# The closing loads of a two-layer mixture-of-experts kernel, issued from two queues instead of one

## The chip, the cores and the metric

The program runs on one core of one Trainium2 chip. The metric is the device time of one execution in microseconds (us), the median of several runs. The engines are TensorE (PE), VectorE (DVE), ScalarE (ACT), GpSimd (POOL) and SyncE (SP). SP computes nothing: it waits on semaphores and issues DMAs. ACT and POOL can issue DMAs too; all of them run on the core's 16 DMA engines.

## The reference

Two layers, each a per-sequence conditioning followed by a mixture of experts, are added to x, which is 4096 tokens of 128 features. The end of the second layer is what matters here. Each token goes to a first and a second choice out of 8 experts, and the two expert rows come back weighted:

```
combine = (g1[:, None] * mask1)[:, :, None] * oh1[:, None, :] + (g2[:, None] * mask2)[:, :, None] * oh2[:, None, :]
expert_out = jnp.einsum('ecf,efh->ech', hmid, w2) + b2[:, None, :]
y = jnp.einsum('nec,ech->nh', combine, expert_out)
shared = jax.nn.silu(x @ sw1 + sb1) @ sw2 + sb2
out = y + SHARED_SCALE * shared
x = x + out
```

## The kernel before

The 4096 tokens lie in SBUF in `acc`, as 32 tiles of 128 tokens. Four tiles make a group, and there are NG = 8 groups. When the expert stage begins, `acc` already holds x and the shared part of the second layer.

The expert stage works on 40 blocks of 256 rows (8 experts, 5 blocks each). PE computes a block, DVE adds the bias into `grp_y` (L1164), and POOL scatters the rows with indirect DMAs (L588) into a DRAM tensor `back1`. It has 4096 rows of first choices and 4096 rows of second choices, in the order of the tokens. The scatters of even blocks count on the semaphore `gy_st[0]`, those of odd blocks on `gy_st[1]`.

The end of the program, which is what is changed, gathers nothing: it reads `back1` in order. It consists of four instruction streams, each in the order in which it is written:

- SP waits until all scatters have landed (L485). Then it issues 16 loads of 256 KB (L488), in the order group 0 first choices, group 0 second choices, group 1 first choices and so on. Both loads of a group g count on one semaphore, `fy_ld[g]`. Behind them SP waits group by group for `f_ac` and issues the 8 stores of `acc` to the output (L491).
- ACT waits for both loads of group g (`fy_ld[g]` at 32) and multiplies the four tiles of second choices by their weights, in place (L764, four ACTIVATEs of 128x128). The last counts on `f_sc`.
- DVE waits for the same semaphore and adds the first choices times their weights to `acc` (L1196, four SCALAR_TENSOR_TENSORs of 128x128). Then it waits for ACT's `f_sc` of this group and adds ACT's four tiles (L1201, one TENSOR_TENSOR of 128x512), which counts on `f_ac`. Only then comes the next group.
- PE and POOL have nothing to do there.

The only other DMA that ACT issues in the whole program is its first, the load of `c0w` (L600). No pool and no scheduler decides anything here: each engine runs its own list.

Of the kernel before, what the change touches and what calls it, by code (L numbers as in the profile page):

```python
# [5 lines left out]
def adaln_moe_two_layers(  # L6
# [44 lines left out]
    S = T // B  # L51
    NSUB = c0_w.shape[0]
    E0, _, F0x2 = f0_gate_up.shape
    F0 = F0x2 // 2
    C0 = F0 // P
    NLANG = c1_b2.shape[0]
    A = c1_w1.shape[1] // NLANG
    E1, _, F1 = f1_w1.shape
    C1 = F1 // P
    TOP_K = 2  # L60
# [8 lines left out]
    NG = NT // G  # L69
# [8 lines left out]
    U = 2  # L78
    UP = U * P
    GPE = CAP // UP  # L80
    NQ = E1 * GPE
# [20 lines left out]
    back1_g = back1.rearrange("(k g i p) h -> k g p i h", p=P, i=G, k=TOP_K)  # L102
# [4 lines left out]
    with ctx:  # L107
        def sb(name, shape, dt=fp32):
            return ctx.enter_context(nc.sbuf_tensor(name, shape, dt))

        def sem(name):
            return ctx.enter_context(nc.semaphore(name))
# [21 lines left out]
        back = [[sb(f"back{k}_{g}", [P, G, H]) for g in range(NG)] for k in range(TOP_K)]  # L134
# [202 lines left out]
        gy_st = [sem(f"gy_st{k}") for k in range(2)]  # L337
# [11 lines left out]
        fy_ld = [sem(f"fy_ld{g}") for g in range(NG)]  # L349
# [25 lines left out]
        def _(sp):  # L375
# [108 lines left out]
            for k in range(2):  # L484
                sp.wait_ge(gy_st[k], 16 * U * (NQ // 2))  # L485
            for g in range(NG):
                for k in range(TOP_K):
                    sp.dma_start(back[k][g][:, :, :], back1_g[k, g]).then_inc(fy_ld[g], 16)  # L488
            for g in range(NG):
                sp.wait_ge(f_ac, g + 1)  # L490
                sp.dma_start(out_g[g], acc[:, g * G:(g + 1) * G, :]).then_inc(o_st, 16)  # L491
# [102 lines left out]
        def _(eng):  # L594
# [104 lines left out]
            for n in range(NG + 2):  # L699
# [9 lines left out]
                if 1 <= n < NG + 1:  # L709
                    k = (n - 1) % 2  # L710
# [47 lines left out]
                q_stage(q, q, last=q == NQ - 1)  # L758


            for g in range(NG):
                eng.wait_ge(fy_ld[g], 16 * TOP_K)
                for i in range(G):
                    ins = sc.activation(back[1][g][:, i, :], back[1][g][:, i, :], ACT.Copy,  # L764
                                        scale=wk[:, 1, g * G + i:g * G + i + 1])
                ins.then_inc(f_sc, 1)
# [438 lines left out]
        def _(pe):  # L1205
# [33 lines left out]
            for n in range(NG + 1):  # L1239
# [11 lines left out]
                if n < NG:  # L1251
                    pe.wait_ge(xT_done, n + 1)
                    if n == 0:
                        pe.wait_ge(ld_c0w, 16)
                        pe.wait_ge(off_ready, 1)
                    _, offs = nc.values_load_multi_w_load_instructions(
                        w0off[0:1, n * GB:(n + 1) * GB], engines=(mybir.EngineType.PE,), min_val=0,
                        max_val=(NSUB - 1) * H, skip_runtime_bounds_check_because="subjects are under NSUB")
                    for b in range(QB):
                        if b == 1 and n >= 3 and n % 2 == 1:  # L1260
                            rank0((n - 3) // 2)
                        for i in range(G):
                            t = i * QB + b
                            last = mm(PS[1 + b][0:S, i * H:(i + 1) * H],  # L1264
                                      xT[n % 2][:, t * S:(t + 1) * S], c0w[:, ds(offs[t], H)],
                                      start=True, stop=True)
                        last.then_inc(pe_c, 1)
# [356 lines left out]
```

## Time and profile before

| | us |
|---|---|
| median of 3 runs | 520.14 |
| lowest and highest run | 518.93 and 521.77 |
| the profiled execution's own time | 520.84 |
| span of the profiled execution, first to last instruction | 518.9 |
| what lies around the span | 1.9 |
| end of the program, from the first closing load (495.54) to the end of the span | 23.3 |

The profile is one execution. Times in its rows are us from the start of the span, and durations marked ns are nanoseconds. A row of the timeline gives the start, the length, the engine, the line, the operation with output and input, the count of instructions merged into the row, and in brackets how long the engine was idle before and what released it. SPq and ACTq are the queues on which SP and ACT issue DMAs: the length of such a row is how long the issue held the issuing engine, not how long the transfer took. PE is busy for 86% of the span as a whole, but that says nothing of the last 25 us, in which it does nothing.

### The profile page before, as it was taken

The numbers are of one execution on the slowest core, as the hardware profiler recorded it, in microseconds if no ns is written. First come the engines' busy times: TensorE is split into PE (matmuls) and PEld (weight loads), VectorE is DVE, ScalarE is ACT, GpSimd is POOL, SyncE is SP. The second block draws the span as 40 slices with busy tenths as digits, with TensorE's granted clock in tenths as the row PEclk, the third lists the DMA queues.
The fourth block names the chain that finished last, engine by engine and source line by source line (L and its number), as shares of the span: only waits on it lengthen the run. The fifth ranks groups of instructions, "written<-read, shape, count | busy, mean of one in ns | idle before, by whom it ended". The sixth has DMA issues, their size and how long they took to land.

```text
span 518.9 us, 10032 instructions
## 1 busy us (share of the span) xinstructions
PE 444.6 (86%) x3126; PEld 383.2 (74%) x3127; DVE 249.5 (48%) x776; ACT 252.7 (49%) x580; POOL 234.3 (45%) x255
## 2 busy tenths in 40 slices
PE   5799788989999989999997899739999999999700
PEld 3688665567777775787876699739999999999700
DVE  1145558856566664255687845303233323332146
ACT  2356662236666653456457334205556555565334
POOL 2006545205555563200646777731565556555600
PEclk8899989999999999999997899959999999999955
DMA  9999981102222214300101111141234333431179
GB/s 235 359 359 342 366 262 41 43 10 78 76 75 73 57 23 142 112 1 1 43 26 42 47 53 46 49 104 42 78 99 143 108 80 110 116 79 31 40 201 287
DMA packets 66129, 58.12 MB, mean 112 GB/s; under 512 B 9484, under 2 KB 53151, under 8 KB 66098
## 3 DMA queue, kind: packets, MB, share of 16 engines
q1 hardware_dynamic: 58402, 44.12, 29.2%
q0 software_dynamic: 7168, 12.56, 7.4%
q10 hardware_dynamic: 528, 1.05, 0.7%
q8 instruction: 17, 0.28, 0.2%
q14 instruction: 14, 0.11, 0.1%
HBM read 30.35 MB, written 29.59 MB: 116 GB/s over the span
## 4 chain that ended last, share of the span: by engine, by line
PE 67%; issue 9%; DVE 8%; POOL 6%; DMA 5%; ACT 3%; SPq 0%; POOLq 0%; DVEq 0%; ACTq 0%
PE PS L1541 14%; PE PS L1207 8%; PE PS L1264 7%; POOL rows L570 5%; PE PS L1465 4%; PE PS L1531 4%; PE PS L1529 4%; PE PS L1530 4%; PE PS L1344 3%; PE PS L1296 3%; PE PS L1305 2%; PE PS L1329 2%; PE PS L1331 2%; PE PS L1330 2%; PE PS L1450 2%
## 5 line engine op out<-in xcount | busy, mean ns | idle before, releaser
L588 POOL DMA_INDIRECT back<-grp_y,grp_i x80 | 79.5, 994 | 72.7 <-DVE grp_y L1164 60.1
L570 POOL DMA_INDIRECT rows<-disp,slot x64 | 63.8, 997 | 65.5 <-DVE slot L1007 46.2
L1541 PE MATMUL PS<-w2r,act 128*128 128x128 f32 x640 | 77.7, 275 | 0.0
L1541 PEld LDWEIGHTS PS<-w2r,act 128*128 128x128 f32 x640 | 74.7, 192 | 0.0
L548 POOL DMA_INDIRECT back<-act,blk_i x48 | 46.9, 976 | 54.2 <-DVE act L960 34.1
L743 ACT ACTIVATE act<-PS,b1r 128x256 f32<-128x256 f32 x160 | 62.8, 475 | 14.6 <-PE PS L1531 14.6
L1164 DVE TENSOR_TENSOR grp_y<-PS,b2r 128x256 f32<-128x256 f32 x40 | 17.0, 425 | 89.7 <-PE PS L1541 84.6
L537 POOL DMA_INDIRECT rows<-disp,slot x32 | 32.0, 1001 | 58.1 <-issue 48.5
L598 ACT ACTIVATE xh<-PS 128x256 fp32r<-128x256 f32 (+1 forms) x48 | 20.1, 419 | 68.5 <-PE PS L1207 68.5
L1529 PE MATMUL PS<-xh,w1h 128*128 128x256 f32 x160 | 48.3, 302 | 0.0
L1531 PE MATMUL PS<-xh,w1l 128*128 128x256 f32 x160 | 45.2, 283 | 0.0
L1530 PE MATMUL PS<-xl,w1h 128*128 128x256 f32 x160 | 44.9, 281 | 0.0
L1264 PE MATMUL PS<-c0w,xT 128*32 x256 | 34.4, 298 | 7.7 <-issue 7.7
L1264 PEld LDWEIGHTS PS<-c0w,xT 128*32 128x32 f32 x256 | 30.0, 121 | 11.1 <-issue 9.3
L695 ACT ACTIVATE act<-PS,sb 128x512 f32<-128x512 f32 x32 | 21.7, 688 | 26.6 <-PE PS L1419 26.2
L1501 PEld LDWEIGHTS PS<-sw,act 128*128 128x128 f32 x256 | 33.7, 214 | 1.2 <-ACT act L695 0.7
L1501 PE MATMUL PS<-sw,act 128*128 128x128 f32 x256 | 34.0, 297 | 0.3 <-DVE acc L1098 0.3
L953 DVE SCALAR_TENSOR_TENSOR act<-PS,blk_x,act 128x256 f32<-128x256 f32 x48 | 23.2, 484 | 20.3 <-ACT act L652 20.3
L1344 PEld LDWEIGHTS PS<-w_dn,act 128*128 128x128 f32 x192 | 26.0, 190 | 9.2 <-issue 8.3
L1344 PE MATMUL PS<-w_dn,act 128*128 x192 | 30.2, 280 | 1.1 <-ACT act L598 1.1
L1530 PEld LDWEIGHTS PS<-xl,w1h 128*128 128x128 f32 x160 | 30.5, 191 | 0.0
L652 ACT ACTIVATE act<-PS,blk_x 128x256 f32<-128x256 f32 x48 | 22.8, 475 | 15.6 <-PE PS L1331 15.6
(237 smaller groups left out, 938.2 us busy)
## 6 DMA issues: line engine op xcount, KB each, us to landing
rows<-zrow SPq DMA_DIRECT2D x32, 260.0 KB, 4.5
grp_x<-rows SPq DMA_DIRECT2D x40, 130.0 KB, 2.4
w_raw<-in_f_gate_up SPq DMA_DIRECT2D x8, 512.0 KB, 9.8
back<-zrow SPq DMA_DIRECT2D x8, 512.0 KB, 7.4
back<-back SPq DMA_DIRECT2D x16, 256.0 KB, 5.1
blk_x<-rows SPq DMA_DIRECT2D x48, 65.0 KB, 1.9
acc<-in_x SPq DMA_DIRECT2D x8, 256.0 KB, 5.6
y0g<-back SPq DMA_DIRECT2D x8, 256.0 KB, 3.1
```

The source lines that it names most:

```text
L548: gp.indirect_dma_start(back0, bass.IndirectOffsetOnAxis(ap=blk_i[c][:, 0:1], axis=0), blk_y[s][:, :], None, bounds_check=last_token, oob_ ...
L570: gp.indirect_dma_start(rows1, bass.IndirectOffsetOnAxis(ap=slot[:, k, t:t + 1], axis=0), disp[:, t, :], None, bounds_check=E1 * CAP - 1, ...
L588: gp.indirect_dma_start(back1, bass.IndirectOffsetOnAxis(ap=grp_i[v % NX][:, u:u + 1], axis=0), grp_y[k][:, u, :], None, bounds_check=last ...
L743: sc.activation(act[k][:, c, 0:UP], PS[1 + k * (C1 // 2) + c // 2][:, (c % 2) * UP:(c % 2 + 1) * UP], ACT.Silu, bias=b1r[e][:, c:c + 1]).t ...
L1207: return nc.tensor.transpose(dst, src, ident[0:k, 0:k])
L1264: last = mm(PS[1 + b][0:S, i * H:(i + 1) * H], xT[n % 2][:, t * S:(t + 1) * S], c0w[:, ds(offs[t], H)], start=True, stop=True)
L1344: last = mm(PS[4 if k == 0 else 7][:, 0:H], blk_aT[k][:, c * P:(c + 1) * P], w_dn[:, ds(off + c * H, H)], start=c == 0, stop=c == C0 - 1)
L1501: last = mm(tile(PS[4], i), tile(act[k][:, c, :], i), sw2[:, c, :], start=c == 0, stop=c == C1 - 1)
L1529: mm(y, high, xh[k][:, 0:UP], start=True, stop=False)
L1530: mm(y, high, xl[k][:, 0:UP], start=False, stop=False)
L1531: last = mm(y, low, xh[k][:, 0:UP], start=False, stop=True)
L1541: last = mm(PS[5 + k][:, u * P:(u + 1) * P], act[k][:, c, u * P:(u + 1) * P], w2r[e][:, c, :], start=c == 0, stop=c == C1 - 1)
```

## The change

SP issues only the eight loads of the first choices. ACT issues the eight loads of the second choices, after it has waited for the same scatters. ACT's eight loads all stand ahead of its first weighting. The semaphores, the sizes, the addresses and the arithmetic are the same.

```diff
             for k in range(2):
                 sp.wait_ge(gy_st[k], 16 * U * (NQ // 2))
             for g in range(NG):
-                for k in range(TOP_K):
-                    sp.dma_start(back[k][g][:, :, :], back1_g[k, g]).then_inc(fy_ld[g], 16)
+                sp.dma_start(back[0][g][:, :, :], back1_g[0, g]).then_inc(fy_ld[g], 16)
             for g in range(NG):
                 sp.wait_ge(f_ac, g + 1)
                 sp.dma_start(out_g[g], acc[:, g * G:(g + 1) * G, :]).then_inc(o_st, 16)
@@ scalar engine, behind the last block of the experts @@
+            for k in range(2):
+                eng.wait_ge(gy_st[k], 16 * U * (NQ // 2))
+            for g in range(NG):
+                eng.dma_start(back[1][g][:, :, :], back1_g[1, g]).then_inc(fy_ld[g], 16)
             for g in range(NG):
                 eng.wait_ge(fy_ld[g], 16 * TOP_K)
```

SP's list at its end before. The rows are the closing loads, two to a group (first and second choices), and the stores.

```order
L488 DMA back_0<-back 128x4x128 x2
L488 DMA back_1<-back 128x4x128 x2
L488 DMA back_2<-back 128x4x128 x2
L488 DMA back_3<-back 128x4x128 x2
L488 DMA back_4<-back 128x4x128 x2
L488 DMA back_5<-back 128x4x128 x2
L488 DMA back_6<-back 128x4x128 x2
L488 DMA back_7<-back 128x4x128 x2
L491 DMA out_x<-acc 128x4x128 x8
```

ACT's list at its end now, from its last work for the experts on. Before, the eight DMA rows were not there, and the ACTIVATE of `back_0` followed the last one of the experts at once.

```order
L742 ACTIVATE act<-PS,b1r 128x256 x8
L763 DMA back_0<-back 128x4x128
L763 DMA back_1<-back 128x4x128
L763 DMA back_2<-back 128x4x128
L763 DMA back_3<-back 128x4x128
L763 DMA back_4<-back 128x4x128
L763 DMA back_5<-back 128x4x128
L763 DMA back_6<-back 128x4x128
L763 DMA back_7<-back 128x4x128
L767 ACTIVATE back_0<-back_0,wk 128x128 x4
L767 ACTIVATE back_1<-back_1,wk 128x128 x4
```

Eight DMAs moved from SP, where each stood in second place of its pair, to ACT, where all of them stand ahead of the weighting of group 0.

## Rows read from the trace of the kernel before

**Rows 1.** Page: span and busy time of the engines.

```profile
span 518.9 us, 10032 instructions
...
PE 444.6 (86%) x3126; PEld 383.2 (74%) x3127; DVE 249.5 (48%) x776; ACT 252.7 (49%) x580; POOL 234.3 (45%) x255
```

**Rows 2.** Chain that ended last, 493 us on: start, length, what.

```profile
493.39 2.09 DMA back<-grp_y,grp_i
...
495.54 0.37 SPq L488
...
495.96 0.50 SPq L488
...
497.05 4.92 DMA back<-back
...
501.99 1.29 ACT back L764 x4
...
503.37 0.69 DVE acc L1201
504.06 1.06 DVE acc L1196 x4
...
514.15 0.69 DVE acc L1201
```

**Rows 3.** Timeline of ACT from 495 us on: groups 0, 1 and 7.

```profile
500.01 1.28 ACT L764 ACTIVATE back<-back,wk 128x128 f32<-128x128 f32 x4 [12.63 <-DMA back<-back]
501.99 1.28 ACT L764 ACTIVATE back<-back,wk 128x128 f32<-128x128 f32 x4 [0.71 <-DMA back<-back]
...
512.56 1.28 ACT L764 ACTIVATE back<-back,wk 128x128 f32<-128x128 f32 x4 [0.28 <-DMA back<-back]
```

**Rows 4.** Views of lines 488, then 491: issue (ns min/median/max), time to landing.

```profile
L488 SPq DMA_DIRECT2D back<-back x16: 366/806/1103, 495.5 to 507.3; - x16
...
DMA to landing us min/median/max: 2.6/5.1/5.5
...
L491 SPq DMA_DIRECT2D out_x<-acc x8: 373/792/922, 508.2 to 514.9; - x8
...
DMA to landing us min/median/max: 3.6/4.4/4.8
```

**Rows 5.** Timeline of SP, single issues: load 5, load 16, store 8.

```profile
497.60 0.86 SPq L488 DMA_DIRECT2D back<-back  x1
...
507.35 0.83 SPq L488 DMA_DIRECT2D back<-back  x1
...
514.87 0.37 SPq L491 DMA_DIRECT2D out_x<-acc  x1
```

**Rows 6.** DMA view: packets started in 495.5:519, 495.5:508.18 and 495.5:504.8, in turn.

```profile
DMA packets 12672, 6.29 MB, mean 268 GB/s; under 512 B 384, under 2 KB 12672, under 8 KB 12672
...
DMA packets 6509, 3.24 MB, mean 255 GB/s; under 512 B 191, under 2 KB 6509, under 8 KB 6509
...
DMA packets 4530, 2.25 MB, mean 242 GB/s; under 512 B 128, under 2 KB 4530, under 8 KB 4530
```

**Rows 7.** Windows of 2 us: the last two columns are DMA share and GB/s.

```profile
495.00:497.00 2.00, 0.00 (x0) 0.00 (x0) 0.00 (x0) 0.00 (x0) 0.00 (x0) 0.50 0.14 37
...
507.00:509.00 2.00, 0.00 (x0) 0.00 (x0) 1.93 (x6) 1.28 (x4) 0.00 (x0) 0.50 1.21 291
...
513.00:515.00 2.00, 0.00 (x0) 0.00 (x0) 1.81 (x6) 0.84 (x3) 0.00 (x0) 0.50 1.15 345
```

**Rows 8.** Timeline of SP, then of ACT, in the first 2 us.

```profile
0.79 0.45 SPq L376 DMA_DIRECT2D acc<-in_x  x1
1.30 0.39 SPq L377 DMA_DIRECT2D w0off<-in_subj  x1
...
0.86 0.86 ACTq L600 DMA_DIRECT2D c0w<-in_c_w  x1
1.76 1.28 ACT L602 ACT_TABLE_LOAD   x1 [0.93 <-issue]
```

## The prediction

> **What bounds the kernel now.** I read the page first: PE is busy 86% of the span [rows 1]. That says nothing of the part that the change touches, so the next view is the chain of waits that ended last, from 493 us on [rows 2]. The reader is to see that PE is gone from it. The last scatter lands, SP issues loads, a group lands at 501.97, ACT weights it, and from 503.37 on the chain runs along DVE without a gap: add ACT's tiles (0.69 us), take the next group's first choices (1.06), and again, up to the add at 514.15. Six periods lie between the adds at 503.37 and 514.15, so one is 10.78 / 6 = 1.80 us. DVE is the bound of that stretch, and ACT is only just ahead of it: ACT waits for a landing before every group [rows 3] and needs 1.28 us of each 1.80.
>
> DMA is nearly a bound too: its engines have a share of 1.15 and more (transfers overlap) at 291 GB/s while loads run and at 345 GB/s once stores do [rows 7]. The last add ends at 514.84, its store is issued at 514.87 [rows 5] and lands 3.6 us later [rows 4], and the span ends at 518.87. The store waits behind two others: a lone transfer of that size takes less (below).
>
> The third view is how long an issue holds the queue. The first issues take 0.37 and 0.50 us [rows 2], but the median of the sixteen is 0.81 [rows 4]: load 5 takes 0.86, and load 16 is held from 507.35 to 508.18 [rows 5]. The packets tell why. All 24 transfers are alike and make 12672 packets, 528 each [rows 6]. When load 16 has been issued (508.18), 16 x 528 - 6509 = 1939 packets are still to be started [rows 6]. I read this as a limit: SP gets rid of a load only when all but some 1930 packets, or 3.7 loads, have been started. That it is the fifth load that first takes longer [rows 5] fits. SP can afford to be held. It computes nothing, and its first store has been ready since 504.06 without setting the end.
>
> **The change part by part.**
>
> *ACT's new wait for the scatters* costs nothing. Behind it stand only the eight loads and the weighting, and ACT is idle for 12.63 us there anyway [rows 3]. SP's same wait ends at 495.5, and ACT's should too.
>
> *SP loses eight issues.* Its first store could go some us earlier than 508.23. It gains nothing at the end: the last store hangs on DVE's last add, and the bytes are the same.
>
> *ACT gains eight issues, ahead of its first weighting.* This is the term that counts. Unlike SP, ACT has work behind its issues, and DVE waits for that work. Before, ACT could start at 500.01. If nothing held it, eight issues of 0.50 + 0.05 us would end at 495.54 + 4.4 = 499.9, just in time. If each queue is held as SP's is now, ACT's eighth load is let go when 8 x 528 - 1930 = 2294 packets of ACT's queue have been started. The two queues share the 16 engines; with equal halves that is 4588 packets in all. In the trace of before 4530 have been started by 504.80 [rows 6], and 58 more take 0.1 us: 504.9. Both queues fill at once now, where SP needed from 495.54 to 495.96 for its second load, so I take off 0.4 for the start: ACT is free at 504.5.
>
> From there by rows: a pause of 0.05, the four ACTIVATEs of group 0 take 1.28 [rows 3], DVE's add starts 0.10 after them (501.99 + 1.28 to 503.37) [rows 2, 3]. That is 505.93, and it ends 0.69 later, at 506.62. DVE has taken group 0's first choices long before. Then seven periods of 1.80 give the end of the last add at 519.22. ACT with 1.28 a group and loads that landed by then stay ahead of DVE, so DVE waits only once, at group 0. Before, this add ended at 514.84: 4.4 us later.
>
> *The last store* wins some back. The stores now come 1.80 us apart with no loads left, and one needs under 0.8 us at 345 GB/s (256 KB), so none queues. The nearest row is the least time to landing of a load, 2.6 us, for the one that met an empty queue [rows 4], against 3.6 of the last store now. I take 2.6, so 1.0 less; the other end is no gain at all, if a write to DRAM takes longer than a read from it. Store issued at 519.25, landed at 521.85, and 0.4 to the end of the span as now (518.87 - 514.87 - 3.6): 522.25, that is 3.4 us more.
>
> *The loads' own rate* is the open price. No row has these loads on two queues. Its bounds are 291 GB/s, as now, and 345, the rate of the stores [rows 7]. By 497 only 0.07 MB have moved (2 us at 37 GB/s) [rows 7]; the other 2.2 MB of the 4588 packets take 6.4 us at 345, which ends at 503.4 instead of 504.9: 1.5 us less. I take the lower rate, since it is measured on the same transfers. A loss is as possible where two queues share unevenly: with 60% for SP's queue ACT would need 2294 / 0.4 = 5735 packets, 2 us later. If ACT's queue is preferred, ACT is free early but the first choices land late. At worst all of ACT's 4224 packets go first, until a little before 504.8; pair 0 then lands near 505.5, DVE needs 1.8 for it, and the first add ends near 507.3, 0.7 later than above.
>
> A rule stands against reading the issues as independent: whether the two issuers hamper each other at the issue itself. In the first 2 us SP issued a small load from 1.30 to 1.69 while ACT's issue ran from 0.86 to 1.72, and neither waited for the other to end [rows 8]. The Trainium skill (Perfetto Trace Analysis, section on the DMA instruction, HWDGE) says that the descriptor generator is locked for exclusive use and that an issue can wait for that lock. By that rule 16 issues of 0.50 us would take turns and end after about 8.5 us, at 504.0; by rows 8 they would not. Either is earlier than the 504.5 of the full queues, so the sum stays.
>
> *Sum.* Span 518.9 + 3.4 = 522.3; with 1.9 around it the profiled execution would go from 520.84 to 524.2. Its own time lies 0.7 above the median of the runs, 520.14, so the forecast for the median is 520.14 + 3.4 = 523.5.
>
> **The rivals.**
>
> 1. *ACT isn't held* (not slower). The eight issues end by 500, before or with the first landing. Against it: SP is held from its fifth load on [rows 5], and nothing in a transfer of the same size on ACT's queue would be different. For it: ACT's one DMA, 1 MB, let it go after 0.86 us and its table load followed at once [rows 8], though that is only one instruction into an empty queue. Then the first pair lands up to 0.4 earlier, DVE's chain moves with it at most, and the DMA engines, busy to the end, give little back: 519.7 to 520.1. The Trainium skill (DMA: Bandwidth & Descriptors, "Issuing engines are not separate DMA queues") says that all issuers share the same 16 engines and that issuing from several saves only the issuer's time. Its result is this rival's, no measurable change, and it says nothing of what the issuer has to do next.
>
> 2. *ACT isn't held and the loads also run at 345 GB/s* (faster). DVE is then the only bound: first landing 499.6, the first add ends about 1.7 later at 501.3 or a little after, seven periods to 513.9, plus 3.0 for the store: 516.9 to 517.3 of span, so 518.1 to 518.6 at the median.
>
> 3. *The limit of 1930 packets is for both queues together*, or SP's queue is preferred (slower still). Then ACT's last load is let go where load 15 or 16 is now, at about 507.3 or at 508.18 [rows 5], 2.8 to 3.7 later than 504.5: 526.3 to 527.2. The rows can't exclude it, as only one queue is ever full in them.
>
> **How the numbers follow.** Main case 0.66, from 522.0 (loads at 345) to 525.5 (60% for SP's queue); rival 3 0.15; rival 1 0.15; rival 2 0.04. The range takes in the main case and rival 3 and leaves rivals 1 and 2 out, 0.19: 521.4 to 527.0. About 0.5%, 2.6 us, is what a measurement of this kernel can tell from no change. Slower by more, above 522.7: rival 3 and four fifths of the main case, 0.68. Within it: the rest of the main case, rival 1 and half of rival 2, 0.30. Faster: 0.02.
>
> **What the profile of the changed kernel would show.** ACT: eight issues from 495.5 on, the first four near 0.5 us, the later ones 1 to 1.8 each, the last ending near 504.5; its first ACTIVATE there and not at 500. It then runs with no wait for a DMA. DVE: first choices of group 0 near 500, then one idle stretch of some 4.5 us before the first add, released by ACT; after it a period of 1.80 and a last add ending near 519.2. Stores land 2.6 to 3 us after issue. The forecast is wrong if ACT's first ACTIVATE comes by 500.5 (rival 1), or after 507 (rival 3), or if the last add doesn't follow ACT's first by 14.7 us.

## The result, and the profile after

The median of 22 runs is 521.53 us against 519.75 us for 22 runs of the kernel before, a difference of 1.8 us. The ratio is 1.004, 95% interval 1.0022 to 1.0058, which is about 2.1 us slower. One run of the changed kernel (528.61) was in a slower state and is left out of the ratio; the median of its other 21 runs is 521.15. The three runs of the kernel before that are shown ahead of the prediction are among its 22 and had a median of 520.14. Timed once more beside the experiments (e9 below), the changed kernel came out at 1.0052 (1.0021 to 1.0084). So the sign was right and the size was a little over half of the 3.4 us forecast.

The length that shows this best is the **closing stretch**: from the issue of the first closing load to the end of the span. It was 518.87 - 495.54 = 23.3 us before. In the profiled execution of the changed kernel (own time 523.92, span 522.0) it is 522.0 - 496.63 = 25.4 us, 2.0 more. That its loads begin 1.1 us later is no part of the change: ahead of them the two programs are the same, and e9 begins them at 493.31.

The timeline from 496 us on, SP and ACT, then DVE's first two and last pieces. It answers to [rows 3] and [rows 2].

```profile
496.63 7.92 SPq L487 DMA_DIRECT2D back<-back  x8
496.64 8.05 ACTq L763 DMA_DIRECT2D back<-back  x8
500.97 1.14 DVE L1199 SCALAR_TENSOR_TENSOR acc<-back,wk,acc 128x128 f32<-128x128 f32 x4 [9.37 <-DMA back<-back]
504.74 7.12 ACT L767 ACTIVATE back<-back,wk 128x128 f32<-128x128 f32 x24 [16.29 <-issue]
506.12 0.69 DVE L1204 TENSOR_TENSOR acc<-acc,back 128x512 f32<-128x512 f32 x1 [4.01 <-ACT back L767]
...
513.64 1.28 ACT L767 ACTIVATE back<-back,wk 128x128 f32<-128x128 f32 x4 [0.29 <-DMA back<-back]
...
518.55 0.69 DVE L1204 TENSOR_TENSOR acc<-acc,back 128x512 f32<-128x512 f32 x1
```

Both loads of group 0 have landed at 500.97, since DVE starts on it there. ACT waits for the same semaphore and doesn't start before 504.74: it is still issuing. DVE then stands idle for 4.01 us before its first add, released by ACT. After that ACT runs 24 ACTIVATEs, six groups, without one wait. The last pair of loads lands at 513.64, 17.0 us after the first issue; in the kernel before it was 512.56 - 495.54 = 17.0 us too [rows 3].

The chain of waits that ended last, in the same stretch. Columns are start, length, what; the group of before is [rows 2].

```profile
498.24 0.53 ACTq L763
...
498.79 1.12 ACTq L763
...
499.94 1.72 ACTq L763
...
501.69 1.56 ACTq L763
...
503.28 1.42 ACTq L763
...
504.74 1.28 ACT back L767 x4
...
506.12 0.69 DVE acc L1204
```

ACT's queue, which wasn't in the chain before, is now the way to the first ACTIVATE. Four issues are free (about 0.5 us each), and the fifth to eighth are held for 1.12, 1.72, 1.56 and 1.42 us.

For comparison, groups 3 and 4 of the kernel before, ACT's weighting and DVE's add:

```profile
505.57 1.28 ACT L764 ACTIVATE back<-back,wk 128x128 f32<-128x128 f32 x4 [0.53 <-DMA back<-back]
506.95 0.69 DVE L1201 TENSOR_TENSOR acc<-acc,back 128x512 f32<-128x512 f32 x1
507.38 1.28 ACT L764 ACTIVATE back<-back,wk 128x128 f32<-128x128 f32 x4 [0.53 <-DMA back<-back]
508.76 0.69 DVE L1201 TENSOR_TENSOR acc<-acc,back 128x512 f32<-128x512 f32 x1
```

There the landings come 1.81 us apart and each add begins 1.38 us after its landing. In the changed kernel DVE has the loads lying ready, and its adds come (518.55 - 506.12) / 7 = 1.78 us apart. So in the kernel before it was the landings that set the pace here, with DVE almost as slow, and a late DVE can make up a little: counted from the first load, its first add is 9.49 - 5.84 = 3.65 us later than before, and its last one ends 3.3 us later.

Packets started in 496:504.7 by queue (q1 is SP's, q10 ACT's), in the form of [rows 6], and two windows, which answer to [rows 7]:

```profile
q1 hardware_dynamic: 2040, 1.02, 44.4%
q10 hardware_dynamic: 1839, 0.92, 41.0%
```

```profile
501.00:503.00 2.00, 0.00 (x0) 0.00 (x0) 1.11 (x4) 0.00 (x0) 0.00 (x0) 0.50 1.21 290
...
513.00:515.00 2.00, 0.00 (x0) 0.00 (x0) 1.93 (x7) 1.62 (x6) 0.00 (x0) 0.50 1.15 345
```

From 501 on, loads on two queues run at 290 GB/s, as on one. When ACT's last issue ended, 4224 - 1839 = 2385 of its packets were still to be started.

The stores' own view, as in [rows 4]:

```profile
L490 SPq DMA_DIRECT2D out_x<-acc x8: 372/373/378, 506.8 to 519.3; - x8
...
DMA to landing us min/median/max: 2.3/3.6/7.2
```

No store is held now, against a median of 0.79 us of issue before. From the end of the last add (519.24) to the end of the span it is 2.8 us, where it was 4.0.

### The profile page after: what moved, and what is told of

Same layout as the page of the kernel before. It is cut to its first block, busy times and chain, and to the rows that moved or that the text cites. A ratio compares the mean times of both kernels' runs of the same rounds, so it can differ in the third digit from the quotient of the medians.

```text
span 522.0 us, 10033 instructions
## 1 busy us (share of the span) xinstructions
PE 445.2 (85%) x3126; PEld 383.5 (73%) x3127; DVE 249.2 (48%) x776; ACT 251.9 (48%) x580; POOL 234.7 (45%) x255
## 4 chain that ended last, share of the span: by engine, by line
PE 68%; issue 9%; DVE 8%; POOL 5%; DMA 4%; ACT 3%; ACTq 2%; POOLq 0%; SPq 0%; DVEq 0%
PE PS L1544 14%; PE PS L1210 8%; PE PS L1267 7%; POOL rows L569 5%; PE PS L1468 4%; PE PS L1534 4%; PE PS L1532 4%; PE PS L1533 4%; PE PS L1347 4%; PE PS L1299 3%; PE PS L1332 2%; PE PS L1308 2%; PE PS L1334 2%; PE PS L1333 2%; PE PS L1453 2%
## 5 line engine op out<-in xcount | busy, mean ns | idle before, releaser
L1267 PEld LDWEIGHTS PS<-c0w,xT 128*32 128x32 f32 x256 | 30.0, 121 | 12.2 <-issue 10.3
L956 DVE SCALAR_TENSOR_TENSOR act<-PS,blk_x,act 128x256 f32<-128x256 f32 x48 | 23.2, 484 | 20.5 <-ACT act L651 20.4
L1532 PEld LDWEIGHTS PS<-xh,w1h 128*128 128x128 f32 x160 | 30.4, 190 | 0.0
```

Of the source, the lines that this page charges most:

```text
L1267: last = mm(PS[1 + b][0:S, i * H:(i + 1) * H], xT[n % 2][:, t * S:(t + 1) * S], c0w[:, ds(offs[t], H)], start=True, stop=True)
L1532: mm(y, high, xh[k][:, 0:UP], start=True, stop=False)
```

## The experiments

Two theories were tested. **Theory 1**: the loss is that ACT comes late to group 0, because its queue holds it while it issues, and DVE waits for it. **Theory 2**: two queues slow the loads themselves. Closing stretch, first weighting and last add are read from each profile, counted in us from the issue of the first closing load.

| kernel | first weighting | last add ends | closing stretch | ratio to before (95%) |
|---|---|---|---|---|
| before | 4.5 | 19.3 | 23.3 | |
| changed | 8.1 | 22.6 | 25.4 | 1.004 (1.0022 to 1.0058) |
| changed again (e9) | 7.9 | 22.4 | 25.1 | 1.0052 (1.0021 to 1.0084) |
| one queue, ACT busy 4.9 us (e1) | 4.8 | 19.3 | 23.0 | 0.9989 (0.9957 to 1.0021) |
| one queue, ACT busy 8.0 us (e5) | 7.9 | 22.4 | 25.1 | 1.0044 (0.9991 to 1.0097) |
| the same, timed again (e10) | 7.9 | 22.4 | 25.1 | 1.0012 (0.9979 to 1.0045) |
| ACT issues 4 loads (e2) | 4.4 | 19.2 | 23.2 | 1.001 (0.9981 to 1.004) |
| ACT issues 6 loads (e6) | 5.1 | 19.6 | 23.1 | 0.9926 (0.9857 to 0.9995) |
| ACT issues 8, four ahead (e11) | 4.3 | 19.6 | 23.0 | 0.9968 (0.9939 to 0.9998) |
| 2 KB runs, two queues (e3) | 4.2 | 18.7 | 21.5 | 0.9969 (0.9936 to 1.0003) |
| 2 KB runs, one queue (e4) | 3.4 | 18.2 | 20.8 | 0.995 (0.992 to 0.9981) |

Each stretch is from one profile, and each ratio is to runs of the kernel before on the same chip. The runs e5 to e8 fell on a chip where the kernel before takes 577.66 us and its single runs differ by up to 10 us, so their ratios say little. The closing stretch, where PE doesn't work, is the same there: e5 and e10 are one kernel on two chips and agree in all three columns. e7 and e8 are given in the text.

**e1: ACT busy, too briefly.** In the kernel before, ahead of ACT's first wait for a load:

```diff
+            for k in range(2):
+                eng.wait_ge(gy_st[k], 16 * U * (NQ // 2))
+            for buf in y0g + nrm:
+                for i in range(G):
+                    sc.activation(buf[:, i, :], ident[:, :], ACT.Copy)
```

> The loads stay on SP's queue as in the kernel before. ACT alone is kept busy after the last scatter: 24 copies of 128x128 into buffers that nothing reads any more, about 7.7 us, before it waits for group 0. This doubles the suspected cost without a second queue. Theory 1 (the change loses because ACT comes late to group 0): ACT's first weighting starts about 8 us after the first load is issued (4.5 before, 8.1 in the changed kernel), DVE idles some 3.5 us before its first add, and the end moves by 1.5 to 2.5 us, as with the change. Theory 2 (two queues slow the loads themselves): an ACT that is late on one queue costs little, under 0.5 us.

The 24 copies took 4.9 us and not 7.7, so ACT was late by only 0.8 us (landing at 4.0, first weighting at 4.8). DVE waited 1.06 us for it, and the last add still ended at 19.3. The size was missed, and the run doesn't separate the two theories, but in its trace a delay of this size costs nothing at the end: DVE at 1.78 us a group catches up with landings 1.81 apart.

**e5 and e10: ACT busy as long as it was held.** The same with 14 copies of 128x512 and 3 of 128x128 into buffers that nothing reads any more. e10 is the same kernel, on a steadier chip.

> As the earlier run that kept ACT busy, but longer, because 24 copies of 128x128 took only 5.0 us and delayed group 0's weighting by 0.8 us. Now 14 copies of 128x512 and 3 of 128x128, about 8.0 us, on ACT between the last scatter and group 0; all loads on SP's queue. Theory 1 (an ACT that is late by itself makes the loss, beyond the slack at the end of before): first weighting about 8.1 us after the first load is issued, DVE idle 3.5 to 4 us before its first add, last add 22.6 us after the first load, and from the first load to the end of the span 25.4 us (23.3 before, 25.4 in the changed kernel, 23.0 with ACT busy for 5.0 us); time 2 us above before. Theory 2 (two queues slow the loads): 23 to 24 us.

> All loads on SP's queue, ACT kept busy for about 8 us ahead of group 0, timed a second time. Theory 1: the same ratio as the changed kernel within the noise (1.003 to 1.005), first weighting at 7.9 us, first load to end of the span 25.1 us. Theory 2 (the second queue as such costs): near 1.000.

Timeline of e10, where SP alone issues loads, and its waits (engine, line, what for: us in total, times, longest):

```profile
494.22 12.72 SPq L488 DMA_DIRECT2D back<-back  x16
497.88 1.14 DVE L1204 SCALAR_TENSOR_TENSOR acc<-back,wk,acc 128x128 f32<-128x128 f32 x4 [8.68 <-DMA back<-back]
502.12 7.10 ACT L772 ACTIVATE back<-back,wk 128x128 f32<-128x128 f32 x24
503.49 0.69 DVE L1209 TENSOR_TENSOR acc<-acc,back 128x512 f32<-128x512 f32 x1 [4.46 <-ACT back L772]
...
515.91 0.69 DVE L1209 TENSOR_TENSOR acc<-acc,back 128x512 f32<-128x512 f32 x1
```

```profile
DVE acc L1209 <- ACT back L772: 4.5, 1, 4.5
```

With one queue for all loads and a late ACT, the trace is that of the changed kernel: first weighting at 7.9, last add ending at 516.60 - 494.22 = 22.4, closing stretch 25.1, as in e9; e5's profile has the same three numbers. In the trace the whole stretch is explained by ACT's delay. The times don't confirm it: theory 1 had asked for 1.003 to 1.005, e10 came out at 1.0012, and the intervals of e5 and e10 hold both no change and the 1.004 of the changed kernel. Beside e10, on the same chip, e9 has the same stretch and yet a median 2.5 us higher (523.31 against 520.84). The intervals of the two ratios overlap, but the means of the twelve single runs differ by 2.0 us, with a 95% interval that I estimate at 0.3 to 3.7. So by the times a part of the loss could have another cause, and that stays open.

**e2: ACT issues four loads, SP the other twelve.**

```diff
             for g in range(NG):
                 sp.dma_start(back[0][g][:, :, :], back1_g[0, g]).then_inc(fy_ld[g], 16)
+                if g >= 4:
+                    sp.dma_start(back[1][g][:, :, :], back1_g[1, g]).then_inc(fy_ld[g], 16)
...
-            for g in range(NG):
+            for g in range(4):
                 eng.dma_start(back[1][g][:, :, :], back1_g[1, g]).then_inc(fy_ld[g], 16)
```

> ACT issues the second choices of groups 0 to 3 only; SP issues those of groups 4 to 7, each behind the first choices of its group. Theory 1 with a limit per queue near four loads: ACT's four issues take 0.5 us each and are over 2.2 us after the first, ACT starts group 0 when it lands (about 4.3 us), DVE never waits long, and the kernel is as fast as before or up to 0.8 us faster. Theory 2: with two queues in the critical first half, the loss of the changed kernel (about 2 us) stays by half or more.

The view of ACT's issues (ns min/median/max):

```profile
L765 ACTq DMA_DIRECT2D back<-back x4: 454/526/528, 496.8 to 498.4; - x4
```

Nothing is held, ACT starts when group 0 lands, and the loss is gone: closing stretch 23.2. Two queues serve groups 0 to 3 here, so theory 2 falls in the trace, as it does by the last pair's landing after 17.0 us with one queue and with two. Nothing is gained either: group 0 lands at 4.4 instead of 4.5.

**e6: ACT issues six loads** (the same edit with 6 for 4).

> ACT issues the second choices of groups 0 to 5, SP those of 6 and 7. By the changed kernel's trace ACT's sixth issue ended 5.0 us after its first, and with four loads (0.5 us each, over after 2.1 us) nothing was held. Theory 1: ACT starts group 0 at 5.0 us, 0.6 after it landed; the first add is late by 0.6, which the queue of stores at the end absorbs; first load to end of the span 23.0 to 23.7 us, the time as before. If instead the limit counts both queues together, ACT with six loads is held about as long as with eight (7 us or more) and the loss is near that of the changed kernel.

```profile
548.42 5.00 ACTq L765 DMA_DIRECT2D back<-back  x6
552.72 1.14 DVE L1201 SCALAR_TENSOR_TENSOR acc<-back,wk,acc 128x128 f32<-128x128 f32 x4 [8.86 <-DMA back<-back]
553.46 2.45 ACT L769 ACTIVATE back<-back,wk 128x128 f32<-128x128 f32 x8 [13.22 <-DMA back<-back]
554.84 0.69 DVE L1206 TENSOR_TENSOR acc<-acc,back 128x512 f32<-128x512 f32 x1 [0.98 <-ACT back L769]
```

ACT's issues end 5.0 us after the first, 0.7 after group 0 landed. DVE waits 0.98 us, and the closing stretch is 23.1. With four, six and eight loads ACT is free at 2.1, 5.0 and 8.1 us: the hold sets in behind the fourth load, and each further load takes 1.5 us on average.

**e7 and e11: eight loads, four of them ahead.**

```diff
-            for g in range(NG):
+            for g in range(4):
                 eng.dma_start(back[1][g][:, :, :], back1_g[1, g]).then_inc(fy_ld[g], 16)
...
                 ins.then_inc(f_sc, 1)
+                if g + 4 < NG:
+                    eng.dma_start(back[1][g + 4][:, :, :], back1_g[1, g + 4]).then_inc(fy_ld[g + 4], 16)
```

> ACT issues all eight loads of the second choices, but only four ahead of its first weighting; each of the other four is issued after the weighting of the group four before it. The two queues and their loads stay as in the changed kernel, only the order on ACT differs. Theory 1: ACT starts group 0 at its landing, 4.4 us, the loss is gone; each issue takes 0.5 us or less out of ACT's spare 0.5 per group; first load to end of the span 22.5 to 23.5 us, the time as before or up to 0.8 us faster, since SP's stores can start at about 8 us and mix with the loads. Theory 2: 25 us.

> Two queues, ACT's second four loads issued between its weightings, timed a second time. Theory 1: ratio 0.997 to 1.001, first load to end of the span 23.0 us, first weighting at 4.4 us. Theory 2: near the changed kernel's ratio.

e7 had a closing stretch of 23.0 too; its ratio, 0.9854 (0.9767 to 0.9942), is from the unsteady chip, and I don't use it. Timeline of ACT in e11:

```profile
498.26 0.40 ACT L767 ACTIVATE back<-back,wk 128x128 f32<-128x128 f32 x1 [12.49 <-DMA back<-back]
498.27 0.43 ACTq L771 DMA_DIRECT2D back<-back  x1
498.57 0.97 ACT L767 ACTIVATE back<-back,wk 128x128 f32<-128x128 f32 x3
500.07 0.40 ACT L767 ACTIVATE back<-back,wk 128x128 f32<-128x128 f32 x1 [0.53 <-DMA back<-back]
```

The same sixteen loads come from the same two queues as in the changed kernel; only where four of them stand on ACT differs, and 2.1 us of closing stretch go (25.1 in e9 to 23.0). This is the cleanest test of theory 1, and the only one that the times bear out: ratio 0.9968 (0.9939 to 0.9998) beside 1.0052 (1.0021 to 1.0084) on the same chip. The medians are 4.1 us apart, more than the 2.1 of the trace.

**e3 and e4: fewer packets for the same bytes.** The scatters put the four tokens of a partition side by side in DRAM, and the loads read them so. e3 has this in the changed kernel, e4 in the kernel before. The edit does the same to the loads of the first layer's results, so the ratios hold both.

```diff
-        back0_g = back0.rearrange("(g i p) h -> g p i h", p=P, i=G)
-        back1_g = back1.rearrange("(k g i p) h -> k g p i h", p=P, i=G, k=TOP_K)
+        back0_g = back0.rearrange("(g p i) h -> g p i h", p=P, i=G)
+        back1_g = back1.rearrange("(k g p i) h -> k g p i h", p=P, i=G, k=TOP_K)
...
-            gp.iota(codes[:, :], pattern=[[-P, NT]], base=FAR, channel_multiplier=-1,
+            gp.iota(codes[:, :], pattern=[[-GP, NG], [-1, G]], base=FAR, channel_multiplier=-G,
```

> The changed kernel, with the scatter tables in another order of rows: the four tokens that a partition of a group takes lie side by side in DRAM, so each closing load has 128 runs of 2 KB instead of 512 of 512 bytes (the loads of the first layer's results too). Bytes and issues are the same. If the limit that holds ACT counts packets: eight loads fit, all eight issues take 0.5 us or less, ACT starts at the first landing, and the kernel is about 2 us faster than before instead of 2 slower. If it counts bytes: ACT is held to about 8 us after the first issue, as in the changed kernel, and the time is above that of before by 1 to 2 us.

> The kernel before with the same order of rows (2 KB runs), all 16 loads on SP. If the limit counts packets: SP is hardly held, the loads end early, the stores no longer queue behind them, the last store lands 2.7 us after the last add instead of 4.0, and the kernel is 1 to 2 us faster than before. Against the run with two queues and the same rows it tells what the second queue is worth once nobody is held: at most the 0.4 us by which the second load of group 0 is issued earlier.

ACT's issues in e3, then SP's in e4, and two windows of e4, one with loads and one with stores:

```profile
L763 ACTq DMA_DIRECT2D back<-back x8: 358/481/712, 492.5 to 496.2; - x8
```

```profile
L488 SPq DMA_DIRECT2D back<-back x16: 338/432/633, 493.4 to 500.8; - x16
```

```profile
501.00:503.00 2.00, 0.00 (x0) 0.00 (x0) 1.97 (x7) 1.68 (x6) 0.00 (x0) 0.50 1.03 394
...
507.00:509.00 2.00, 0.00 (x0) 0.00 (x0) 1.97 (x6) 1.34 (x5) 0.00 (x0) 0.50 1.15 345
```

Eight loads of the same 256 KB leave ACT after 4.2 us, none held over 0.71. What holds an issue is the count of packets and not the bytes: when the eighth is issued, 261 of ACT's 1152 packets and 0.49 of its 2.10 MB have been started. The 1.6 MB left are more than the 2.10 - 0.92 = 1.2 MB down to which the changed kernel's ACT was held.

The loads run at 394 GB/s in this window, and at 365 to 404 in others of e3 and e4. The closing stretch is 3.9 us shorter in e3 than in the changed kernel and 2.5 shorter in e4 than before, and e4 is faster than both kernels of this study: 0.995 (0.992 to 0.9981). One queue has the shorter closing stretch here, by 0.7 us. In e4's profile group 0's two loads, first in line, land at 3.4; in e3's they share the engines with each other and with what is queued behind, and land at 4.1, when DVE starts. I had expected the second queue to land them earlier. This is one profile of each: with one queue and 512-byte packets the same landing came anywhere from 3.6 to 4.5 us (e5, e10, e1, before), and the times of e3 and e4 don't tell the two apart.

**e8: GpSimd takes half of the second adds,** on top of e4: POOL adds the second choices of groups 0, 2, 4 and 6 behind DVE's weighted add of the first, DVE keeps the odd groups.

The part of the edit on GpSimd; SP's waits and DVE's skipping of the even groups are left out:

```diff
...
+            for g in range(0, NG, 2):
+                pool.wait_ge(f_st, g // 2 + 1)
+                pool.wait_ge(f_sc, g + 1)
+                a = acc[:, g * G:(g + 1) * G, :]
+                gp.tensor_tensor(a, a, back[1][g][:, :, :], ALU.add).then_inc(f_ap, 1)
...
```

> The kernel before with 2 KB runs in the closing loads (all on SP's queue) and, in addition, GpSimd adds the second choices of groups 0, 2, 4 and 6 (its add of the same shape took 1.28 us in the first layer), DVE those of the odd groups. DVE then needs 2 x 1.13 + 0.69, about 2.95 us for two groups instead of 3.55; the last add ends 16 us after the first load instead of 18.2 and the stores become the bound: 4.2 MB at 385 GB/s and 2.1 MB at 345 take 17.0 us and about 2.5 around them, so first load to end of the span 19.5 to 20 us against 20.8 with the rows alone; the time 3 to 3.5 us below before. If GpSimd and DVE hamper each other at SBUF, DVE's operations get longer than 0.35 and 0.69 us and nothing is gained over the rows alone.

Groups of instructions of DVE in the closing stretch (busy us, mean ns), e8 and then e4:

```profile
L1204 DVE SCALAR_TENSOR_TENSOR acc<-back,wk,acc 128x128 f32<-128x128 f32 x32 | 12.2, 447 | 10.6 <-DMA back<-back 10.6
```

```profile
L1196 DVE SCALAR_TENSOR_TENSOR acc<-back,wk,acc 128x128 f32<-128x128 f32 x32 | 9.1, 345 | 8.4 <-DMA back<-back 8.4
```

DVE's 32 weighted adds take 12.2 us instead of 9.1. The mean hides where: 28 of them are as short as ever (median 344 ns), and the four that meet one of GpSimd's four adds are long, one of them 0.65 us and three 1.35. The second add of GpSimd and the weighted add that meets it:

```profile
563.47 1.31 POOL L598 TENSOR_TENSOR acc<-acc,back 128x512 f32<-128x512 f32 x1 [2.79 <-DVE acc L1204]
563.57 1.35 DVE L1204 SCALAR_TENSOR_TENSOR acc<-back,wk,acc 128x128 f32<-128x128 f32 x1
```

All four end 0.14 to 0.15 us after GpSimd's add does: DVE's operation is held until GpSimd's is over. The 3.1 us lost are more than the 2.8 that DVE was freed of, four adds of 0.69. The last add ends 19.2 us after the first load, 1 us later than in e4. Its ratio, 1.0041 (0.9981 to 1.0101), is from the unsteady chip and settles nothing; its profile also has SP waiting 5.5 us for PE's queue at the very end, which no other had and which I leave unexplained.

**e9: the changed kernel again.**

> The changed kernel itself, beside the two below on one chip, since the last group of runs fell on a chip where the whole kernel takes about 577 us and single runs differ by several us. Every theory: first load to end of the span 25 to 25.5 us in the trace, 2 us over the kernel before; ratio 1.003 to 1.005.

The closing stretch is 25.1 us, as expected, and the ratio of 1.0052 is just above the expected 1.005. DVE's wait for ACT is 3.93 us, against 4.01 in the first profile.

## Why the prediction was right, and where its size was off

- *The number*: 523.5 was forecast for the median, from 521.4 to 527.0, and 521.53 came out. The main case began only at 522.0; the range reached 0.6 us lower, for which the text gave no reason, and the median lies in that piece. That the range holds it is luck: without the run of 528.61 it would be 521.15 and outside.
- *What bounds the kernel*: nearly right. DVE's chain of adds did carry the delay on, but the 1.80 us a group that the text read as DVE's own pace was that of the landings (1.81); DVE alone needs 1.78. So from the first add to the last it is 518.55 - 506.12 = 12.43 us, where the text had 12.6, and of the 3.65 us by which the first add was late 0.3 was made up by the last. "Ready since 504.06" for the first store was a misreading: group 0's add ended at 501.38 + 0.69 = 502.07. Nothing rests on it.
- *ACT's issues as the term that counts*: right in mechanism, shown by e11 (move four issues, the loss goes) and by the traces of e5 and e10 (an ACT late for another reason gives the same stretch), but too large in size. The text had ACT free 504.5 - 495.54 = 9.0 us after the first load; it was 8.1 (504.69 - 496.63). The term that was mis-sized is the limit of 1930 packets. It was read from one queue and carried over to two, but ACT's queue let go with 2385 packets still to be started. So 2040 + 1839 = 3879 packets in all were enough, not 4588. At 290 GB/s and 528 packets to 256 KB, the difference of 709 packets is 1.2 us. The 0.4 taken off for a quicker start was worth at most 0.1: the two queues had started 3879 packets 8.1 us after the first load, and the one queue of before 3808 after 8.0 us. So 0.3 of it was too much, and 1.2 - 0.3 is the 0.9 us by which ACT was free earlier than forecast. The limit isn't one fixed count either. At the end of loads 6 to 16 of before between 1895 and 2031 packets were waiting; at the end of loads 5 to 8 of the changed kernel it was 2157 to 2226 on SP's queue and 2196, 2166, 2274 and 2385 on ACT's. Why a queue takes some 200 to 450 more when a second one is full stays open.
- *The loads' rate* with two queues, left open between 291 and 345 GB/s: from 501 on it is 290, the value taken. The queues shared nearly evenly (2040 and 1839 packets), as the sum assumed.
- *The last store*: right in kind, 0.3 too dear. The text had 3.03 us from last add to end of span, where 2.76 were measured and 4.03 before. That all stores land after 2.6 to 3 us was wrong: their median is 3.6 and the longest 7.2, since the first ones are issued (from 506.84) while loads are still to land (the last pair at 513.64).
- *The sum*: 0.9 (ACT's issues) + 0.2 (DVE's pace) + 0.3 (last store) = 1.4 us is what the text had too much, 3.4 against 2.0 in the trace. So the time fell within the 0.5% that a few runs can't tell from no change, which the text had given 0.30, less than half of what it gave to a larger loss.
- *Rival 1* (ACT isn't held): fell, four issues were held for 1.1 to 1.7 us. *Rival 2* fell with it. *Rival 3* (one limit for both queues together): fell. ACT's 2385 waiting packets alone are more than the 1930 that would have been the limit of both, and SP had some 2184 more; and e6 was not held like eight loads.
- *The lock rule* of the Trainium skill (Perfetto Trace Analysis, section on the DMA instruction, HWDGE), by which issues would take turns: the first four issues of both queues ran side by side at 0.37 to 0.53 us each and were over after 2.1 us. Eight in turn at 0.5 would have needed 4. The trace doesn't agree with issues that take turns as wholes; whether some part of an issue takes turns it can't show.
- The other rule of the Trainium skill that was named, that a second issuer saves only issue time (DMA: Bandwidth & Descriptors, "Issuing engines are not separate DMA queues"), agrees with the 290 GB/s. It doesn't reach to the cost found here, that the issuer has work of its own behind the held issues.

## What to carry to other kernels

A DMA that is issued from a computing engine is cheap as long as its queue has room, and holds the whole engine when it has none: put no more loads ahead of the engine's work than the queue takes (four of 528 packets each here), and issue the rest between its operations. Look for issues in the trace that take longer than the first ones, and ask what stands behind them on that engine. Where issues are held, count the packets: longer contiguous runs in DRAM shortened the closing stretch to 20.8 us here, and no way of spreading the issues brought it below 23.0.

## What the runs showed of the hardware

- The hold counts packets, per queue: an issue is let go with 1895 to 2031 waiting on a lone queue (before) and with 2157 to 2385 on each of two (changed). The fifth load of 528 packets is the first to be held, and eight loads of 144 packets (e3) are not.
- The first four issues of SP and of ACT run at the same time (changed), for 0.37 to 0.51 us on SP, as on SP alone before, and 0.45 to 0.53 on ACT.
- An issue of ACT runs beside its own arithmetic. In e11 it takes from 498.27 to 498.70, while ACTIVATEs written ahead of it run from 498.26 to 499.54, and the group as a whole takes 1.28 us as before.
- In windows of 2 us, loads in 2 KB runs moved 365 to 404 GB/s once under way (e3, e4) and loads in 512-byte runs 290 to 295 from 501 on (changed) or 503 on (before); stores in 512-byte runs moved 345.
- An add on GpSimd holds a SCALAR_TENSOR_TENSOR of DVE that meets it until 0.14 us after its own end: 1.35 us instead of 0.34 (e8). The others aren't slowed.
